# Key stores of a windowed attention split by the term they read, with a completion count for each term

## The reference

```python
qkv = xw @ qkv_w + qkv_b                      # xw: normed pixels by window
logits = q_win * SCALE @ swapaxes(k_win)      # means over the 64 pixels of a window
r_idx = top_k(logits, 4)
k_sel, v_sel = kv_pix[r_idx]                  # 4 windows, 256 keys
attn = softmax(einsum('npqhd,npkhd->nphqk', qh * SCALE, kh))
out = einsum('nphqk,npkhd->npqhd', attn, vh) + lepe
x = x + out @ wo_w + wo_b
```

## Time and profile before

| | |
|---|---|
| Median of three executions | 4986.31 us (4976.98 to 4998.5) |
| Profiled execution, its own time | 4985.82 us |
| Span of the profile | 4984.0 us |
| TensorE matmul busy | 3849.6 us, 77% of the span |
| VectorE busy | 2427.0 us, 49% |
| ScalarE busy | 2301.1 us, 46% |
| GpSimd busy | 1261.4 us, 25% |
| Moved by DMA | 484.86 MB, 97 GB/s over the span |

### The profile page before, as it was taken

How to read it: one execution, slowest core, us unless ns; L and a number is a source line. 1 busy time by engine, 2 the same in 40 slices (tenths; PEclk the granted TensorE clock), 3 DMA queues, 4 the chain that set the end, 5 groups by cost and what they waited for, 6 DMA issues and landing times. The chain is left out here.

```text
span 4984.0 us, 164012 instructions
## 1 busy us (share of the span) xinstructions
PE 3849.6 (77%) x52926; PEld 2748.4 (55%) x52926; DVE 2427.0 (49%) x4011; ACT 2301.1 (46%) x5133; POOL 1261.4 (25%) x4158
## 2 busy tenths in 40 slices
PE   4247788687778778777877777788949799999889
PEld 1124565455555545555544554556612388888789
DVE  2254575475556556545655654665625233333311
ACT  1125565555555555555555555567813233333300
POOL 1022343243334324333433433344400000000000
PEclk9998888888888888887888888889955699999955
DMA  2324434343433434343344334333259543444486
GB/s 77 106 61 100 97 91 104 97 97 91 102 93 89 102 97 95 89 104 91 87 103 100 91 91 104 95 83 67 41 76 141 90 106 84 107 103 88 103 184 166
DMA packets 778340, 484.86 MB, mean 97 GB/s; under 512 B 483369, under 2 KB 752042, under 8 KB 773130
## 3 DMA queue, kind: packets, MB, share of 16 engines
q1 hardware_dynamic: 718210, 407.83, 37.1%
q10 hardware_dynamic: 59360, 67.44, 4.7%
HBM read 264.35 MB, written 209.19 MB: 95 GB/s over the span
## 5 line engine op out<-in xcount | busy, mean ns | idle before, releaser
L554 POOL COPY Ksel<-Kexp 96x128 int32 x3136 | 925.3, 337 | 1793.2 <-PE ps L1182 1640.0
L917 DVE TENSOR_REDUCE Mx<-ps 128x2 f32<-128x512 f32 x1568 | 1060.1, 687 | 497.3 <-PE ps L1160 490.0
L766 ACT ACTIVATE Pr<-ps 128x1024 f32<-128x1024 f32 x784 | 800.9, 1022 | 973.9 <-PE ps L1182 824.4
L1180 PE MATMUL ps<-Qbd,Ksel 96*128 96x128 bf16 x6272 | 901.5, 233 | 24.9 <-issue 23.9
L1182 PE MATMUL ps<-MT,each 84*128 84x128 bf16 x6272 | 901.8, 233 | 0.0
L687 ACT ACTIVATE Vsel<-Vpx 64x72 f32 x3136 | 815.4, 260 | 136.4 <-DMA Vpx<-v_dram 66.2
L1160 PE MATMUL ps<-Ksel,Qbd 96*128 96x256 bf16 x3136 | 644.2, 289 | 139.1 <-POOL Ksel L554 94.3
L1180 PEld LDWEIGHTS ps<-Qbd,Ksel 96*128 96x128 bf16 x6272 | 661.4, 106 | 110.6 <-issue 101.2
L1182 PEld LDWEIGHTS ps<-MT,each 84*128 84x128 bf16 x6272 | 662.4, 106 | 102.8 <-issue 95.0
L1199 PE MATMUL ps<-Pr,Vsel 128*9 128x64 f32 x25088 | 530.9, 228 | 118.9 <-ACT Vsel L687 66.7
L1199 PEld LDWEIGHTS ps<-Pr,Vsel 128*9 128x9 f32 x25088 | 386.9, 94 | 310.3 <-issue 309.6
(11 more groups left out here) (166 smaller groups left out, 3604.3 us busy)
## 6 DMA issues: line engine op xcount, KB each, us to landing
q_dram<-Pq SPq DMA_DIRECT2D x336, 112.0 KB
k_dram<-Pk SPq DMA_DIRECT2D x336, 112.0 KB
Kexp<-k_dram ACTq DMA_DIRECT2D x112, 336.0 KB, 4.4
Qbd<-q_dram SPq DMA_DIRECT2D x224, 168.0 KB, 4.2
Vpx<-v_dram ACTq DMA_DIRECT2D x112, 252.0 KB
s_dram<-S SPq DMA_DIRECT2D x8, 2048.0 KB, 12.7
Sin<-s_dram SPq DMA_DIRECT2D x32, 512.0 KB, 5.7
z_dram<-Zs SPq DMA_DIRECT2D x128, 128.0 KB, 4.0
```

The source lines that it names most:

```text
L554: nc.gpsimd.tensor_copy(dst[:, w, :, k, :], src[:, :, bass.ds(win[k] * (PX // 2), PX // 2)])\
L766: nc.scalar.activation(Pr[k][:].rearrange("q c p h x -> q (c p h x)"), ps[:, ST0 + 2 * k:ST0 + 2 * k + 2, :].rearrange("q a b -> q (a b)") ...
L917: nc.vector.tensor_reduce(Mx[u % 2][:, 2 * half:2 * half + 2, w], ps[:, half, :].rearrange("q (p k) -> q p k", p=2), AX.X, ALU.max).then_i ...
L1180: mm(out, Ksel[u % 2][:, w, p, 2 * c:2 * c + 2, :].rearrange("r k x -> r (k x)"), query(u, w, p), start=True, stop=False)
```

## The change

The single count `k_stored` becomes three, one for each term. The three stores of term 0 are issued right behind the six query stores; the other three (two of term 1, one of term 2) stay where the key stores were. `first_k` waits for the three stores of term 0, `second_k` for the two of term 1, `third_k` on VectorE for the one of term 2. `load_k` waits for all three counts. Bytes, shapes and number of the transfers stay the same.

```diff
-            def store_k(e, i):
-                hold(sp, "sp", k_part2, e * NWIN + i + 1)
-                for n, (_, part) in enumerate(TERMS):
-                    sp.dma_start(k_dram[at(e), :, n, :, i * ROW:i * ROW + ROW].rearrange("a b c x -> (a b) c x"),
-                                 Pk[:, part, :]).then_inc(k_stored, 16)
+            def store_k(e, i, part):
+
+                ready, done = ((k_part0, k0_stored), (k_part1, k1_stored), (k_part2, k2_stored))[part]
+                hold(sp, "sp", ready, e * NWIN + i + 1)
+                for n, (_, term) in enumerate(TERMS):
+                    if term == part:
+                        sp.dma_start(k_dram[at(e), :, n, :, i * ROW:i * ROW + ROW].rearrange("a b c x -> (a b) c x"),
+                                     Pk[:, part, :]).then_inc(done, 16)
...
                 if behind:
                     store_q(e, u - 1)
+                    store_k(e, u - 1, 0)
                 if prev:
                     rsums_to_dram(g - 1, (u - 1) % 2)
...
                 if behind:
-                    store_k(e, u - 1)
+                    store_k(e, u - 1, 1)
+                    store_k(e, u - 1, 2)
                 if not last and LAST <= u < UNITS - 1:
                     load_vh(e, u - LAST)
...
             def first_k(t):
                 hold(act, "act", k_ready, t + 1)
-                hold(act, "act", k_stored, t * (6 * 16))
+                hold(act, "act", k0_stored, t * (3 * 16))
...
             def second_k(t):
                 hold(act, "act", k_res, t + 1)
+                hold(act, "act", k1_stored, t * (2 * 16))
...
             def load_k(e, b, i):
-                hold(act, "act", k_stored, (e * NWIN + i + 1) * (6 * 16))
+                hold(act, "act", k0_stored, (e * NWIN + i + 1) * (3 * 16))
+                hold(act, "act", k1_stored, (e * NWIN + i + 1) * (2 * 16))
+                hold(act, "act", k2_stored, (e * NWIN + i + 1) * 16)
...
             def third_k(t):
                 hold(dve, "dve", k_part1, t + 1)
+                hold(dve, "dve", k2_stored, t * 16)
```

More of the change, by code:

```diff
@@ L219, in attention @@
         q_stored = sem("q_stored")
-        k_stored = sem("k_stored")
+        k0_stored = sem("k0_stored")
+        k1_stored = sem("k1_stored")
+        k2_stored = sem("k2_stored")
         vs_stored = sem("vs_stored")
@@ L427, in _ @@
                 store_q(0, i)
-                store_k(0, i)
+                for part in range(3):
+                    store_k(0, i, part)
                 store_vs(0, i)
```

## The result

| | before | changed kernel |
| --- | --- | --- |
| median of 4 runs | 4985.7 us | 4937.6 us |
| lowest to highest | 4977.0 to 4998.5 | 4930.6 to 4948.2 |
| ratio, 95% interval | | 0.9903 (0.9875 to 0.9931) |
| profiled execution: own time, span | 4985.8, 4984.0 | 4939.1, 4937.3 |
| TensorE's mean granted clock | 0.853 | 0.866 |

The change makes the kernel 48 us faster, 1.0%; the forecast was 4949 us, 37 us faster, 0.7%.

The account below looks back on a forecast made before the run. No engine is full; waits bound the kernel, chiefly `first_k` waiting for key stores. A pair gains 45.5 us and loses 40.2, so 5.3, 37 us for seven: 4985.8 to 4949 us, range 4855 to 5050.

Parts of the forecast that it names:

- The drain of the stores sets `Rb`: At the reload of inverted sums: the sums' store lands only after the query stores drain, `Rb` 11.1 us after the first.
- The term of 4.2 + 1.4 = 5.6 us: Added delay of `Rb`: 4.2 us for three stores at 82 GB/s, 1.4 us for `Kexp` falling into the drain.
- Issuing three more stores costs nothing: On SyncE, which issues a store each 0.7 us and idles from 1283.83 to 1287.26 ahead of the sums' store.
- The clock, 2.3 us on top: TensorE idles behind `normalise` and its clock falls: 2.3 us extra in each of steps 2, 3, 4 and 6.
- The rival that the clock stays up: TensorE's idle time at w = 6 does not drop the clock: 116 us less, 4870 us; chance 0.2.
- The wait at `first_k` goes whole, 37.8 us a pair: ScalarE's 264.6 us wait for key stores goes, as term 0's stores are issued some 20 us earlier.
- `VH`, 8.7 us in step 8 and 1.0 us left in step 7: VectorE's wait for value rows: step 8 gains 7.2 plus 1.5 of clock; step 7 keeps 1.0 us.
- Step 5 pays nothing: Later `normalise` costs 0 in step 5, since the next step starts when ScalarE's `Vpx` load has landed.
- `second_k` and `third_k` don't wait: `second_k` has 13.05 us for stores needing 2.8 to 5.5; `third_k` comes later and needs one store more.
- hidden drain: Three stores drain in 2.2 us, as fast as issued, no clock loss: 242 us gained, 4744 us; chance 0.05.
- dearer drain: A term 0 store costs 2.7 us beside `Kexp`, three take 8.2: 72 us slower, 5058 us; chance 0.18.
- The rival of the wait that moves on: Stores of terms 1 and 2 take 16.4 us, `second_k` waits 3.3 us in five steps: 5066 us; chance 0.07.

Follow-up runs that it names:

- experiment 5: Changed kernel with term 1's two stores also ahead of the sums' store, five key stores there and one at the end: 5143.3 us, ratio 1.0329.
- experiments 7 and 10: Changed kernel with `q_dram` and `k_dram` laid out for 32 x 4 row stores: 4601.7 us; the same plus `Vpx` loads in halves: 4501.7 us.
- Experiment 1: Changed kernel with term 0's stores back in their old place, all six in term order, waits per term kept: 4861.4 us, ratio 0.9754.
- experiment 9: Changed kernel with each `Vpx` load cut into two loads of 64 partitions, stores and layouts as they are: 4821.5 us, ratio 0.9676.
- experiment 2: Changed kernel's store places, but `first_k` waits for all six key stores as before: 5001.9 us, ratio 1.0040 against the kernel before.

## Why the prediction was right

- **"The drain of the stores sets `Rb`"**: shown. No, three and five key stores ahead of the sums' store give 11.1, 15.9 and 18.6 us to `Rb` (changed kernel and experiment 5), and with stores that drain faster three cost 0.6 to 1.1 us (experiments 7 and 10). The term of 4.2 + 1.4 = 5.6 us measured 4.8, the sum of 20.1 us to `normalise` 19.4. Its two parts can be told apart: in step 7, where `Kexp` lay in the drain already, the three stores alone moved `Rb` by 3.2 us (means 12.5 and 15.7), and in steps 1 to 6 by 4.8 with `Kexp` new beside them. The wait there is 328.8 us and not the 250 named as a sign: the 250 left out steps 1 and 5, and step 5 waits as long as the others (6.77 us in pair 2). One difference in that passage is off: 20.1 less 16.9 is 3.2 us for step 1, not 3.1, which is 0.7 us over seven pairs.
- **Issuing three more stores costs nothing**: held. SyncE issues them in 3.1 us and then still waits 6.0 us (1301.22 to 1307.23 in step 3) for the sums to land.
- **The clock, 2.3 us on top**: the sign it named is there, the clock at 0.50 behind `normalise` (0.64 on the mean of 10 us) and full beside the query stores. The size was somewhat smaller: from `normalise` to the next step the median of steps 1 to 4 and 6 of the seven pairs is 8.46 us and was 6.86, 1.6 us and not 2.3. The rival that the clock stays up fell.
- **The wait at `first_k` goes whole, 37.8 us a pair**: right in size, wrong in what it was credited to. The forecast gave the gain to stores issued 20 us earlier. Experiment 1 shows that waiting for term 0 alone, with the stores in their old place, takes away 214 of the 265 us, and the move then costs more than the last 50 are worth.
- **`VH`, 8.7 us in step 8 and 1.0 us left in step 7**: the term that was mis-sized. Left are 2.9 us in step 7 and 3.1 in step 8 (means of seven), 5 us a pair more than I had. The forecast counted the three stores that no longer stand ahead of `VH` and took `Vpx` as no longer slowed by them. It did not ask what `Vpx` does to `VH`, and that is what is left: experiment 9 has the same late `Rb` with `Vpx` in halves, and no wait for `VH` in steps 7 and 8. So the delay of `Rb` by itself does not make this wait. In the step lengths: step 8 gave 4.1 us and not 8.7.
- **Step 5 pays nothing**: held, if not as told. `normalise` comes later there too, but `Vpx` has landed by then, so its wait at the start of step 6 (7.59 us in pair 2, 51.9 us in all) is gone but for 3.0 and the new one stands in its place.
- **What made up for `VH`**: step 5 gave 1.1 us more than the forecast, steps 6 and 7 together 2.5, steps 2 to 4 0.7. The sum for a pair came out at 5.2 us against 5.3, closer than its parts deserve: `VH` alone was off by about as much as the whole sum, so that the net fits is luck. Over the span there were some 10 us more, from the eighth pair, which the forecast left out (its first step 26.1 to 19.8 us), and the rest of the kernel.
- **`second_k` and `third_k` don't wait**: held, but for two short waits at `third_k`, 2.9 us in all. The margin was smaller than the 13.05 us against 2.8 to 5.5 of the forecast: experiment 2 shows that the last three stores land some 2.5 us after `first_k` would come, and `second_k` runs about 4 us behind it. The rival of the wait that moves on was closer than 0.07 said, though it did not happen.

The rivals of the hidden drain and the dearer drain fell with the 15.9 us.

## What to carry to other kernels

When one count covers six transfers, first split the wait, by what each reader needs, and leave the transfers in place: that alone was worth 124 us here and cost two small waits, while moving transfers ahead of a load that somebody waits for handed 76 us of it back. Before reordering a queue, look at the DMA share of a stretch that holds one kind of transfer: 0.27 with nothing else under way was the work of a quarter of the engines, and changing the shape of the transfer gave 330 us. With that the order was still worth 54 us; with the `Vpx` load cut as well, no order beat the old one and that of the change lost 40. A transfer can be taken out of one place only by putting it into another; ask who stands behind it there.

## What the runs showed that I had not expected

- The same 112 KB store moved at 82 GB/s with its rows as 4 x 32 and at 138 to 140 GB/s as 32 x 4, at which point SyncE's 0.7 us per issue was the limit.
- Behind nine stores in a row the two loads of `Qbd` took 8.63 us to issue (median 8.3), against 3.29 in the changed kernel and 1.7 with `Vpx` in halves. ScalarE's load of `Vpx` was issued among them (at 1338.11), so the stores' own share is not isolated.
- With eleven stores ahead `Rb` took 6.6 us from its issue to its reader instead of 3.4, though it is issued only when the store of the sums has landed; the load of `Vpx` was issued beside or ahead of it each time.
- The loads of `Vpx` in one piece cost 116 us in all (experiment 9), while 70 us of waits carried their name.
